# First attention of a two-block transformer: a guard and a copy dropped, a subtraction moved from VectorE to ScalarE and GpSimd, queries projected ahead of the key scores

## The reference

```python
x = x + tanh(g_xattn[0]) * L0_xattn(layernorm(x), ctx, ctx)   # the first attention
x = x + tanh(g_ffn[0]) * L0_ffn(layernorm(x))                 # top-k memory; starts with layernorm(x) @ patterns.T
x = x + tanh(g_xattn[1]) * L1_xattn(layernorm(x), ctx, ctx)   # rotary, masked
x = x + tanh(g_ffn[1]) * L1_ffn(layernorm(x))                 # 16 experts and a shared one

def L0_xattn(x0, x1, x2):
    q, k, v = heads(x0 @ Wq.T + bq), heads(x1 @ Wk.T + bk), heads(x2 @ Wv.T + bv)
    attn = softmax(-0.25 * q @ k.T)
    return merge(attn @ v) @ Wp.T + bp
```

## Time and profile before

| | us |
|---|---|
| median of 3 runs | 747.66 |
| lowest and highest run | 741.65, 748.21 |
| the profiled execution: its time | 744.32 |
| its span | 742.2 |
| TensorE busy (multiplications) | 659.8 |
| VectorE busy | 454.9 |
| ScalarE busy | 354.1 |
| GpSimd busy | 237.5 |

### The profile page before, as it was taken

The page is one execution under the profiler, slowest core; times in us unless marked ns, Lnnn a source line. Parts: engine busy times, 40 slices in busy tenths (PEclk is TensorE's granted clock), DMA queues, the critical chain, the costliest instruction groups (busy, mean ns, idle before and its releaser), DMA issues.

```text
span 742.2 us, 13201 instructions
## 1 busy us (share of the span) xinstructions
PE 659.8 (89%) x4816; PEld 535.0 (72%) x4816; DVE 454.9 (61%) x944; ACT 354.1 (48%) x780; POOL 237.5 (32%) x250
## 2 busy tenths in 40 slices
PE   5898987989997867775999988999987999999998
PEld 3666655768875545553566656999876999999997
DVE  3778977111107566767687635548896877778703
ACT  3267555656662233142566675323266556666400
POOL 6655512700000230035866221000134455555400
PEclk9999988999999988996999999999999999999999
DMA  7965740592000043205767643000001565566313
GB/s 260 267 170 147 208 116 1 217 418 77 0 0 1 2 163 118 46 1 129 138 151 146 139 74 149 23 1 2 1 0 63 180 224 202 202 201 204 114 29 113
DMA packets 61347, 87.17 MB, mean 117 GB/s; under 512 B 17256, under 2 KB 50664, under 8 KB 60264
## 3 DMA queue, kind: packets, MB, share of 16 engines
q1 hardware_dynamic: 60496, 85.90, 38.5%
q10 hardware_dynamic: 800, 0.59, 0.3%
HBM read 63.54 MB, written 18.73 MB: 111 GB/s over the span
## 4 chain that ended last, share of the span: by engine, by line
PE 71%; DVE 15%; issue 6%; ACT 3%; POOL 2%; DMA 2%; ACTq 0%; DVEq 0%; POOLq 0%
PE ps L1087 69%; DVE keep L2005 2%; DMA keep<-in_x 1%; DVE keep L2016 1%; PE ps L1093 1%; DVE keep L2013 1%; DVE keep L1998 1%; ACT vp L765 1%; DVE G L2216 1%; DVE mcol L1813 1%; DVE hhi_s L2143 1%; DVE keep L1827 1%; ACT keep L793 0%; DVE att L2141 0%; DVE keep L1833 0%
## 5 line engine op out<-in xcount | busy, mean ns | idle before, releaser
L1087 PE MATMUL ps<-keep 128*128 128x120 bf16 (+7 forms) x473 | 60.6, 257 | 19.9 <-DVE keep L2005 14.5
L1087 PE MATMUL ps<-thi,whi 128*128 128x256 f32 x256 | 73.7, 288 | 3.9 <-POOL tlo L695 2.1
L1087 PE MATMUL ps<-thi,wlo 128*128 128x256 f32 x256 | 72.4, 283 | 0.0
L1087 PE MATMUL ps<-tlo,whi 128*128 128x256 f32 x256 | 72.2, 282 | 0.0
L887 ACT ACTIVATE ps<-ps 128x256 f32<-128x256 f32 x128 | 47.6, 372 | 41.0 <-PE ps L1087 40.9
L1087 PEld LDWEIGHTS ps<-keep 128*128 128x128 bf16 (+1 forms) x473 | 34.1, 112 | 41.2 <-DVE keep L2005 26.2
L995 ACT ACTIVATE att<-ps 128x512 f32<-128x512 f32 x48 | 28.6, 596 | 67.4 <-PE ps L1087 67.1
L559 POOL TENSOR_TENSOR kbr<-khi,keep 128x616 fp32r<-128x616 f32 x32 | 39.8, 1266 | 61.2 <-PE ps L1087 58.9
L1087 PE MATMUL ps<-xhi,phi 128*128 128x512 f32 x128 | 51.4, 401 | 2.9 <-ACT ps L887 2.9
L1087 PEld LDWEIGHTS ps<-thi,whi 128*128 128x128 f32 x256 | 48.6, 190 | 5.9 <-issue 3.5
L1087 PE MATMUL ps<-xhi,plo 128*128 128x512 f32 x128 | 50.6, 396 | 0.0
(11 more groups left out here) (250 smaller groups left out, 1849.3 us busy)
## 6 DMA issues: line engine op xcount, KB each, us to landing
q_rows<-qhi SPq DMA_DIRECT2D x32, 256.0 KB, 2.6
big<-in_piw SPq DMA_DIRECT2D x4, 2048.0 KB, 12.5
qpair<-q_rows SPq DMA_DIRECT2D x8, 768.0 KB, 5.7
qhead<-q_rows SPq DMA_DIRECT2D x8, 768.0 KB, 7.5
q_rows<-qlo SPq DMA_DIRECT2D x16, 256.0 KB, 2.8
att<-in_wg SPq DMA_DIRECT2D x8, 512.0 KB, 3.8
att<-in_wu SPq DMA_DIRECT2D x8, 512.0 KB, 4.8
att<-in_wd SPq DMA_DIRECT2D x8, 512.0 KB, 5.5
```

The lines of the kernel that those rows point to most:

```text
L1087: return pe.matmul(out, lhsT, rhs, start=start, stop=stop, skip_group_check=True)
```

## The change

Three things. `divide` in the first attention no longer takes the greater of the sum and 1e-30 before the reciprocal, and `stats_second` writes its result where it is wanted and not through a copy. The low part of the second norm's tokens, for batches 0 to 5, is made by GpSimd: ScalarE copies the transpose unrounded from PSUM to SBUF (`copy_unrounded`, tile xraw), behind `maxima_out`, and GpSimd subtracts; batches 6 and 7 stay with VectorE. And in layer 0 TensorE projects the queries ahead of the first key scores, ScalarE takes them ahead of the exponentials, and key scores 4 and 5 stand behind `project_out` and `second_rows`.

```diff
@@ gpsimd
             def inv_std_second(k):
-                pool.wait_ge(fmv_done, k + 1)
+                pool.wait_ge(fmv_done, 2 * k + 2)
+            def low_part(k):
+                part = xlo[:, :, bslice(k)]
+                pool.wait_ge(xt2_done, k + 1)
+                pool.tensor_tensor(part, xraw[:, :, bslice(k)], words(xhi)[:, :, bslice(k)], ALU.subtract
+                                   ).then_inc(xlo_done, 1)
                     add_bias(n)
+                    if layer == 0 and n >= 2:
+                        low_part(n - 2)
                     if n > lo:
                         inv_std_second(n - 1)
@@ scalar
+            def copy_unrounded(k, bank):
+                act.activation(xraw[:, :, bslice(k)], ps[:, bank, :].rearrange("p (c t) -> p c t", c=DC), ACT.Copy
                                ).then_inc(xt2_done, 1)
+                    if n + 2 < hi and layer == 0:
+                        high_queries(n + 2)
                     exponentials(n, (0, 1))
                     if n == 2 * B - 1:
                         round_shared(0)
-                    if n + 2 < hi and layer == 0:
-                        high_queries(n + 2)
...
                     if n + 2 < hi:
                         maxima_out(n + 2)
+                    if n - 2 >= lo and layer == 0:
+                        copy_unrounded(n - 2, R_BANK + 1)
@@ tensor
+                    if m < hi and layer == 0:
+                        project_q(m)
                     key_scores(n, (0, 1))
-                    if m < hi:
-                        if layer == 0:
-                            project_q(m)
-                        else:
-                            swap_pairs(m)
+                    if m < hi and layer == 1:
+                        swap_pairs(m)
...
                             if m >= 5:
-                                pe.wait_ge(xlo_done, m - 4)
+                                pe.wait_ge(xt2_done, m - 4)
                             first_rows(m)
...
-                    key_scores(n, (4, 5))
+                    if layer == 1 or m >= hi:
+                        key_scores(n, (4, 5))
                     if n > lo:
                         project_out(n - 1)
                     if m < hi:
                         if layer == 0:
                             second_rows(m)
+                            key_scores(n, (4, 5))
@@ vector
                 for t in range(2):
-                    dve.bn_aggr(fag[:, t, :], fbn[:, t, :]).then_inc(faggr_done, 1)
-                dve.wait_ge(faggr_done, k * 2 + 2)
-                dve.tensor_copy(fmv[:, tiles(b), :], fag).then_inc(fmv_done, 1)
+                    dve.bn_aggr(fmv[:, 2 * b + t, :], fbn[:, t, :]).then_inc(fmv_done, 1)
...
-                dve.tensor_scalar(den, turned4[:, :, :, HD], TINY, None, ALU.max).then_inc(div_step, 1)
-                dve.wait_ge(div_step, 3 * i + 1)
-                dve.reciprocal(rec, den).then_inc(div_step, 1)
-                dve.wait_ge(div_step, 3 * i + 2)
+                dve.reciprocal(rec, turned4[:, :, :, HD]).then_inc(div_step, 1)
+                dve.wait_ge(div_step, 2 * i + 1)
...
                     divide(n, 0)
-                    if n >= 2:
-                        low_part(n - 2, R_BANK + 1)
```

More of the change, by code:

```diff
@@ L111, in flamingo_kernel @@
         fbn = keep(2 * 6).rearrange("p (t k) -> p t k", k=6)
-        fag = keep(2 * 2).rearrange("p (t k) -> p t k", k=2)
         fmv = keep(T // P * 2).rearrange("p (t k) -> p t k", k=2)
@@ L125, in flamingo_kernel @@
         scaled = tk[:, 512:768]
-        den, rec = (tk[:, at:at + 16].rearrange("p (a t) -> p a t", a=2) for at in (768, 784))
+        rec = tk[:, 768:784].rearrange("p (a t) -> p a t", a=2)
         tied, above, above_lo, eqb = (keep(64).bitcast(BF16) for _ in range(4))
@@ L174, in flamingo_kernel @@
         Vpad = vp(B * H * 32).rearrange("p (b h m) -> p b h m", b=B, h=H)
+        xraw = vp(DC * T, XLO_AT).rearrange("p (c t) -> p c t", c=DC)
         midT = vp(T // P * D, XLO_AT).rearrange("p (b c q) -> p b c q", b=B, c=DC)
@@ L267, in flamingo_kernel @@
         cleared, prepared, tanh_done, bpt_done = sem("cleared"), sem("prepared"), sem("tanh_done"), sem("bpt_done")
-        fstat_done, faggr_done, fmv_done = sem("fstat_done"), sem("faggr_done"), sem("fmv_done")
+        fstat_done, fmv_done = sem("fstat_done"), sem("fmv_done")
         fveps_done, frstd_done = sem("fveps_done"), sem("frstd_done")
@@ L724, in round_xt @@
                 act.wait_ge(xt2_ps, k + 1)
-                act.activation(xhi[:, :, bslice(k % B)], ps[:, bank, :].rearrange("p (c t) -> p c t", c=DC), ACT.Copy
+                ins = act.activation(xhi[:, :, bslice(k % B)], ps[:, bank, :].rearrange("p (c t) -> p c t", c=DC), ACT.Copy)
+                if k >= B - 2:
+                    ins.then_inc(xt2_done, 1)
+            def copy_unrounded(k, bank):
+                act.activation(xraw[:, :, bslice(k)], ps[:, bank, :].rearrange("p (c t) -> p c t", c=DC), ACT.Copy
                                ).then_inc(xt2_done, 1)
@@ L1281, in attend @@
                         else:
-                            pe.wait_ge(xlo_done, n - 2)
+                            pe.wait_ge(xt2_done, n - 2)
                         transpose_second(n - 2, R_BANK + 1, xn2[:, n % 2])
@@ L1745, in stats_second @@
                 for t in range(2):
-                    dve.bn_aggr(fag[:, t, :], fbn[:, t, :]).then_inc(faggr_done, 1)
-                dve.wait_ge(faggr_done, k * 2 + 2)
-                dve.tensor_copy(fmv[:, tiles(b), :], fag).then_inc(fmv_done, 1)
+                    dve.bn_aggr(fmv[:, 2 * b + t, :], fbn[:, t, :]).then_inc(fmv_done, 1)
             def low_part(k, bank):
                 dve.wait_ge(xt2_done, k + 1)
+                if k == B - 2:
+                    dve.wait_ge(xlo_done, B - 2)
                 dve.tensor_tensor(xlo[:, :, bslice(k % B)], ps[:, bank, :].rearrange("p (c t) -> p c t", c=DC),
@@ L1820, in divide @@
                 if n >= B:
-                    dve.wait_ge(div_step, 3 * 2 * B + i - 2 * B + 1)
+                    dve.wait_ge(div_step, 2 * 2 * B + i - 2 * B + 1)
                     dve.wait_ge(proj_ps, n)
@@ L1828, in divide @@
                 dve.wait_ge(half_read, i + 1)
-                dve.tensor_scalar(den, turned4[:, :, :, HD], TINY, None, ALU.max).then_inc(div_step, 1)
-                dve.wait_ge(div_step, 3 * i + 1)
-                dve.reciprocal(rec, den).then_inc(div_step, 1)
-                dve.wait_ge(div_step, 3 * i + 2)
+                dve.reciprocal(rec, turned4[:, :, :, HD]).then_inc(div_step, 1)
+                dve.wait_ge(div_step, 2 * i + 1)
                 dve.tensor_tensor(scaled.rearrange("p (t a d) -> p a t d", a=2, d=HD), turned4[:, :, :, 0:HD],
                                   rec.unsqueeze(3).to_broadcast([P, 2, S // 32, HD]), ALU.mult).then_inc(div_step, 1)
-                dve.wait_ge(div_step, 3 * i + 3)
+                dve.wait_ge(div_step, 2 * i + 2)
                 if n > 0:
@@ L1868, in attend_first @@
                         low_queries(n + 2)
-                    if n + 2 < B:
                         maxima(n + 2, 0)
```

## The result

| | before | after |
|---|---|---|
| median of 20 runs, us | 747.93 | 752.18 |
| lowest and highest | 741.65, 751.47 | 747.36, 757.2 |
| the profiled execution: time, span | 744.32, 742.2 | 757.2, 755.4 |

What follows compares the result with a forecast made beforehand. The prediction took VectorE's queue to bound the kernel before, and TensorE and ScalarE in turn after. Profiled 744.32 us plus 3.6 for the later last projection plus 2.4 for one clock fall gave 750.3 us, range 742 to 758.

Steps and rivals of the forecast that it cites:

- The bound before: First attention: VectorE's queue sets the batch's 11.5 us; dropped work is worth 1.17 us a batch, 7.0 in six.
- The batches: New order, TensorE and ScalarE in turn: 13.0 us in batches 2 and 3, 12.0 in 4 and 5, before 11.5.
- the long piece of ScalarE: Exponentials 4 and 5 and normalisations lose the projection as cover: 4.53 us from scores to values, 3.53 with one normalisation.
- VectorE's slack: VectorE's low queries are ready 1.1 us before the projection's turn; this slack swallows VectorE's saving.
- GpSimd's subtraction: Moved low part, 128x512, ahead of inv_std_second in GpSimd's queue: 1.4 us taken, between ends of 1.28 and 1.56.
- The end: Last batch: normalise_second(6) waits for inv_std_second(6) behind low_part(5); last projection at 128.6 for 125.00, 3.6 us later.
- The start: Batch 0: project_q(2) starts at 29.5 in place of 31.40; values, rows and scores follow some 1.5 us earlier.
- The clock step: TensorE falls to half clock behind project_q, slowing projection and second rows: 2.4 us a fall, one fall taken.
- The total: Whole kernel: 744.32 + 3.6 + 2.4 = 750.3 us, range 742 to 758; main forecast's chance 0.63.

Runs made afterwards that it cites:

- e3_drops_only: The kernel before with only the guard and the copy dropped; 743.86 us, ratio 0.9937 to before.
- e5_pairs45_back: The changed kernel with key scores 4 and 5 back ahead of the projection out, queries still first; 746.09 us, ratio 0.9990 to before.
- e6_normalise_late: The changed kernel with ScalarE's normalise(n + 4) moved from between two exponentials to behind the raw copy; 747.54 us, ratio 1.0018 to before.
- e2_order_only: The kernel before with only the new order on TensorE and ScalarE; guard, copy and VectorE's low part kept; 753.35 us, ratio 1.0077 to before.
- e8_low_part_only: The kernel before with only the low part of batches 0 to 5 moved to ScalarE and GpSimd; 746.53 us, ratio 1.0020 to before.
- e4_second_norm_first: The changed kernel with GpSimd running inv_std_second(6) ahead of low_part(5) in batch 7; 748.99 us, ratio 0.9998 to before.
- e1_old_order: The changed kernel with the old order on TensorE and ScalarE; guard and copy dropped, low part moved; 744.66 us, ratio 0.9969 to before.
- e7_best: The changed kernel with the old order, and inv_std_second(6) ahead of low_part(5) on GpSimd in batch 7; 739.76 us, ratio 0.9870 to before.
- e7_again: The same kernel as e7_best, timed again in a second group; 741.92 us, ratio 0.9884 to before.

## Why the prediction was right

**The bound before.** The prediction has VectorE's queue setting every batch; the runs bear that out in part. Relieved of 0.59 us (e3_drops_only), the kernel won 0.57 a batch on the mean, but 1.12 in batch 3 and 0.08 in batch 4. The chain without a pause that the prediction read is that of batch 3; in the same chain the two batches from 49.03 to 71.94 belong to TensorE with short waits. The second bound was near, TensorE at 10.98 us, so the 1.17 of relief could have given 0.5 to 0.6 even with the old order.

**The batches.** Worked out were 13.0 us with two normalisations and 12.0 with one; measured are 13.10, 13.11 and 12.12. The sum from the scores to the values was 4.53, measured 4.50. The second values of batch 5 were put 3.3 us behind those of the earlier trace rows; they stand at 104.62, of which 1.3 come from a later start of the whole loop (29.98 against 28.67 in the earlier trace rows), so 3.1. That the long piece of ScalarE is the reason was argued then and is shown now, by e5_pairs45_back and e6_normalise_late. Between the second values of batches 0 and 5 the order cost 5.1 us in all (62.03 against 56.92) where 4.8 were worked out.

**VectorE's slack.** The saving was to be swallowed. e2_order_only shows it: all the old work, the same distances. The scaling beside GpSimd's subtraction did take 1.08 us (69.44) and not 0.44, in three batches, and it made no difference to the sum, in the new order. The Trainium skill (Perfetto Trace Analysis, Optimizing Scalar/DVE Operations) says that GpSimd and VectorE share a read port of SBUF, so that moving work from one to the other might not help; the trace agrees. In the old order the move gave 0.08 in batch 3, where TensorE was by then near its bound, and where VectorE had no slack it cost: 1.13 us in batch 5 of e8_low_part_only.

**GpSimd's subtraction** took 1.264 to 1.278 us, at the low end (1.28) of the bounds and not the 1.4 chosen. The tile view of the changed kernel:

```profile
L577 POOL TENSOR_TENSOR xlo<-vp,xhi x6: 1264/1269/1278, 69.0 to 125.9; 128x512 fp32r<-128x512 f32 x6
```

**The end.** Predicted: the last projection 3.6 us later. From the loop's start it is 4.56 later (100.89 against 96.33 us), so the sum was 1.0 too small. The part that was mis-sized most is the end itself, from the second values of batch 5 to the last projection: put at 0.3 more than before, it took 1.5 more (26.25 against 24.76 us). In the frame of before the exponentials at 123.79 stand at 122.5 (put at 121.9), the second normalisation ends at 128.6 (put at 128.1), and the transposes and their copy needed 0.9 at half clock where 0.5 was put. The mechanism, the factors behind the subtraction, is shown by e4_second_norm_first, which undoes it and takes 2.8 us from the last distance.

**The start** was put at a gain of 1.5 us. In the profiles the first rows and the second values of batch 0 lie 14.65 us apart before and 12.61 after; but e1_old_order, with the old order, has 13.00, and e2_order_only, with the new, 12.62. So the order gives 0.4. Against the profiled execution the gain was real and even 2.0. The rest is the fall of the clock in the earlier trace rows (3.15 for project_q), which e3_drops_only shares (14.77) and e1_old_order and e7_best don't. The second execution of e7_best, e7_again, has it (3.42 for project_q, 14.65 us), so one and the same code runs with and without it. All in all three of six profiles with project_q behind the first scores of batch 0 have the fall and none of six with it ahead; whether the order keeps it away is not shown by so few. The step was mis-sized, by taking a stretch at half clock wholly for a price of the order.

**The clock step failed in its place.** One more fall of 2.4 us was put behind project_q in batches 1 to 5. None of the five profiles with the new order there (after, e2, e4, e5, e6) has one; the windows of e2_order_only, where TensorE was busy for 19.37 of 24 us, show the full clock:

```profile
60.00:84.00 24.00, 19.37 (x154) 13.56 (x152) 20.63 (x54) 15.14 (x33) 13.40 (x20) 1.00 0.62 169
```

The changed kernel's falls came at 108.9, 119.2 and 129.4: in batches 6 and 7, which have no project_q and no rows, each as the projection ran behind scores and values, and at the seam, behind the new wait. The kernel before has falls of its own, at the start, at 103.4 and at 124.0; from 26 to 136 us of the span the mean granted clock is 0.92 before and 0.95 after. Windows of the changed kernel:

```profile
108.00:113.00 5.00, 4.97 (x28) 3.03 (x28) 0.86 (x3) 2.40 (x5) 1.82 (x3) 0.66 0.35 74
```

The projection at 108.69 took 3.37 us in it, between the 1.93 of full clock (73.41) and the 3.78 of the earlier trace rows. The fall at the seam is missing in e4_second_norm_first, but not in e7_best with the same edit.

**The total.** Without the step that failed the sum would have been 747.9 on the profiled time, 3.6 up; measured are 4.7 by the ratio. The number came closer than its parts deserved, and that is luck: the clock step, 2.4 too much, stood against an end that was 1.2 too small, batches 0.3 too small, and a start gain of which 1.1 was not the order's. In the profiles the loop is 4.56 longer; beside an execution of before without the fall at the start (1.6 us of the earlier trace rows) it would be 6.2. The interval of the ratio, 3.1 to 6.4 us, holds both. That interval also answers the prediction's sentence that less than 1% can't be told from no change: with 20 runs a side 0.6% could. The profiled run of before is 3.6 below the median of its 20 runs. Of the 13.2 us between the two spans 7.3 lie behind the last projection (624.5 against 617.2), in stages that the change doesn't touch, and 6.6 of these in one stretch: from the second attention's projection at 433.73 us before, 439.47 after, to the first small product of the last stage (L1585 at 459.79, L1601 at 472.12) it is 26.1 us before and 32.7 after. Windows of the changed kernel, then of before:

```profile
440.00:480.00 40.00, 34.33 (x276) 26.50 (x275) 16.79 (x39) 21.74 (x41) 5.84 (x13) 0.79 0.29 88
```

```profile
435.00:470.00 35.00, 29.85 (x291) 23.43 (x291) 18.25 (x44) 21.39 (x41) 5.85 (x13) 1.00 0.27 95
```

The medians follow the loop more than these stretches: the last projection plus 622 us, a figure fitted to them, gives the median of every kernel to within 2.4 us, e2_order_only excepted (747.7 for 753.35). For that one kernel the difference stays open.

## What to carry to other kernels

On in-order queues, look for what runs beside an engine's long piece before moving anything: two pairs of scores, moved behind the projection that ran beside ScalarE's 3 us, cost 1.4 us in a batch with two normalisations, more than all that VectorE was spared. Work that is moved to an idle engine is free for the engine and not for its queue; put it behind what another engine waits for, as the 2.8 us at the last batch show. Look too at what it will run beside: GpSimd's 1.27 us of subtraction made one VectorE scaling a microsecond longer (e8_low_part_only). When three edits go together, time each alone: here the dropped guard and copy were worth 0.5 to 0.6%, with the moved subtraction, the old order and the mended queue 0.7 to 1.3%, and together with the new order less than nothing.

## What was not expected of the hardware

TensorE kept its full clock over two batches with 19.37 of 24 us busy and waits of up to 1.02 us (e2_order_only), and fell in batches 6 and 7 of the changed kernel, which has shorter waits (0.45 and 0.20 us before the scores at 106.76 and 107.90, 0.20 before those at 118.06) but only products of 77 and 98 rows in the 4 us before the fall. Which of the differences decides, no run here shows. The clock's falls differ from one execution to the next in stages with the same instructions (e7_best and e7_again at the start of the loop), and between 434 and 472 us of the span the stretch with them took 6.6 us more than the one without. GpSimd's subtraction of 128x512 took 1.27 us where VectorE's took 0.58, and it stretched a VectorE product of 128x256 from 0.44 to 1.08 us, once to 1.43.
